# Routed experts: the order of the output weighting and of the inner product's rounding on ACT

## The reference, cut to what matters

```
g = einsum('ech,eih->eci', xb, w_gate)      # 32 experts, 192 rows, 512 -> 256
u = einsum('ech,eih->eci', xb, w_up)
inter = silu(g) * u                         # the inner product's operand
yb = einsum('eci,ehi->ech', inter, w_down)  # 256 -> 512
y = yb[eid, pos] * w_slot[:, None]          # each row weighed by its token's routing weight
routed = y.reshape(-1, K, Hd).sum(axis=1)   # added to the token's row
```

## Time and profile before

| what | us |
|---|---|
| median of 3 runs (1690.84 to 1692.87) | 1692.7 |
| the profiled execution's own time | 1691.99 |
| its span | 1690.2 |
| busy in the span: PE | 1483.3 (88%) |
| busy: DVE | 1112.2 (66%) |
| busy: ACT | 1028.2 (61%) |
| busy: POOL | 767.1 (45%) |

### The profile page before, as it was taken

The page is one execution under the profiler, slowest core; times in us unless marked ns, Lnnn a source line. Parts: engine busy times, 40 slices in busy tenths (PEclk is TensorE's granted clock), DMA queues, the critical chain, the costliest instruction groups (busy, mean ns, idle before and its releaser), DMA issues. The chain is left out here.

```text
span 1690.2 us, 26016 instructions
## 1 busy us (share of the span) xinstructions
PE 1483.3 (88%) x8434; PEld 1232.9 (73%) x8436; DVE 1112.2 (66%) x2284; ACT 1028.2 (61%) x2108; POOL 767.1 (45%) x659
## 2 busy tenths in 40 slices
PE   5999969899994589999999999995999869999994
PEld 4877758777773477887887887774887758778773
DVE  4659857777773256666666675664649857777773
ACT  5762447777773266666667666753762537777773
POOL 0123235555653475666556556420113225556563
PEclk9999979999998789999999999997999989999998
DMA  7736358889994111111111110115655448999994
GB/s 268 239 128 205 107 187 267 253 256 259 266 253 79 64 39 51 38 38 63 38 44 45 63 38 32 32 38 179 212 175 158 139 152 255 269 255 266 268 258 72
DMA packets 94599, 255.57 MB, mean 151 GB/s; under 512 B 19153, under 2 KB 20113, under 8 KB 86193
## 3 DMA queue, kind: packets, MB, share of 16 engines
q1 hardware_dynamic: 71984, 202.58, 35.8%
q0 software_dynamic: 22528, 51.92, 14.4%
HBM read 185.70 MB, written 68.76 MB: 151 GB/s over the span
## 5 line engine op out<-in xcount | busy, mean ns | idle before, releaser
L1032 DVE TENSOR_TENSOR e_w_lo<-e_raw,e_w_hi 128x1024 fp32r<-128x1024 f32 x192 | 233.6, 1218 | 108.7 <-ACT e_w_hi L947 100.5
L947 ACT ACTIVATE e_w_hi<-e_raw 128x1024 fp32r<-128x1024 f32 x192 | 202.6, 1056 | 29.2 <-PEq L270 20.8
L1548 POOL TENSOR_SCALAR t_prob<-t_prob,t_inv 128x128 f32<-128x128 f32 (+7 forms) x128 | 112.0, 875 | 221.7 <-DVE t_inv L1455 221.7
L1122 PE MATMUL e_ps_gate<-e_xt,e_w_hi 128*128 128x384 f32 x512 | 161.3, 378 | 38.6 <-DVE e_w_lo L1032 38.5
L899 POOL DMA_INDIRECT e_xg<-htab,e_gather_idx x128 | 140.0, 1093 | 63.5 <-issue 39.3
L910 POOL DMA_INDIRECT x_after_ffn<-e_y,e_add_idx x64 | 104.4, 1631 | 114.8 <-DMA x_after_ffn<-e_y,e_add_idx 92.1
L910 POOL DMA_INDIRECT out<-e_y,e_add_idx x64 | 104.7, 1637 | 104.3 <-DMA out<-e_y,e_add_idx 83.8
L1122 PE MATMUL e_ps_up<-e_xt,e_w_hi 128*128 128x384 f32 x512 | 151.8, 361 | 0.0
L353 POOL TENSOR_SCALAR d_inter<-d_inter 128x512 f32<-128x512 f32 x32 | 26.5, 827 | 267.8 <-DVE d_inter L518 267.6
L1350 ACT ACTIVATE t_prob<-a_wide,t_neg_max,a_q_scale 128x128 f32<-128x128 f32 (+7 forms) x128 | 106.5, 832 | 54.0 <-DVE t_neg_max L1449 53.8
L1122 PEld LDWEIGHTS e_ps_gate<-e_xt,e_w_hi 128*128 128x128 f32 x512 | 99.0, 193 | 48.6 <-issue 28.9
(11 more groups left out here) (222 smaller groups left out, 4476.9 us busy)
## 6 DMA issues: line engine op xcount, KB each, us to landing
e_raw<-in_w_experts SPq DMA_DIRECT2D x64, 1536.0 KB
htab<-d_h SPq DMA_DIRECT2D x16, 1024.0 KB, 5.3
d_x<-in_x SPq DMA_DIRECT2D x16, 512.0 KB, 6.8
d_xs<-in_x SPq DMA_DIRECT2D x32, 256.0 KB, 3.5
x_after_ffn<-d_xs SPq DMA_DIRECT2D x32, 256.0 KB, 3.2
q_x<-x_after_ffn SPq DMA_DIRECT2D x32, 256.0 KB, 3.1
t_res<-x_after_ffn SPq DMA_DIRECT2D x32, 256.0 KB, 2.6
x_after_attention<-t_res SPq DMA_DIRECT2D x32, 256.0 KB, 2.0
```

What stands on the lines that cost most here:

```text
L947: act.activation(w_hi[u][:, cols], raw[u][:, cols], ACT.Copy).then_inc(hi_ready, 1)
L1032: dve.tensor_tensor(w_lo[u][:, cols], raw[u][:, cols], w_hi[u][:, cols].bitcast(F32), ALU.subtract).then_inc(lo_ready, 1)
L1122: pe.matmul(out, w[0][:, c, cols], xt[u][:, c, :, :], start=c == 0, stop=False)
L1548: pool.tensor_scalar(prob[:, u, 0:width(i)], prob[:, u, 0:width(i)], inv[:, u:u + 1], 1.0, ALU.mult, ALU.mult).then_inc(p_ready, 1)
```

## The change

On ACT the weighting of the outputs of the expert behind moves ahead of the rounding of the inner product. `weigh` gets a parameter that could do the halves separately; both calls give it both halves. Nothing is added or left out, and no other engine's stream changes.

```diff
-                def weigh(i, u):
+                def weigh(i, u, halves):
                     e = 2 * i + u
-                    act.wait_ge(y_free, e + 1)
-                    act.wait_ge(col_done, e + 1)
-                    act.activation(add_idx[u][:, :], slots[:, bass.ds(2 * e, 2)], ACT.Copy)
-                    for q in range(2):
+                    if 0 in halves:
+                        act.wait_ge(y_free, e + 1)
+                        act.wait_ge(col_done, e + 1)
+                        act.activation(add_idx[u][:, :], slots[:, bass.ds(2 * e, 2)], ACT.Copy)
+                    for q in halves:
                         act.wait_ge(d_ready, 2 * e + q + 1)
...
                     gate(i, u)
                     unload_up(i, u)
+                    if behind:
+                        weigh(pi, nu, (0, 1))
                     split_inner(i, u)
-                    if behind:
-                        weigh(pi, nu)
                     if ahead:
                         split(ni, nu, 2)
...
-                weigh(E // 2 - 1, 1)
+                weigh(E // 2 - 1, 1, (0, 1))
```

## The result

The changed kernel takes 1711.97 us (median of 4 runs, 1708.39 to 1718.31), the kernel before 1692.51 (median of 4, 1690.84 to 1692.87). The ratio is 1.0108, 95% interval 1.0091 to 1.0126: slower by 1.1%, where 1.5% faster was forecast, and outside the stated range. The profiled execution took 1709.90 us, its span is 1708.1 us, 17.9 us longer than before.

A forecast was written before the change was run, and what follows sets the result against it. It took the ACT-DVE ring, 8.97 us a step, as the bound; with DMA-limited steps of 8.70 us, 8.8 + 6.7 + 9.7 = 25.2 us come off 1691.99, giving 1666.8, plus 0.7: 1667.5 us. Range 1648 to 1690.

The forecast's parts named there:

- The ring: ACT and DVE waiting on each other in the routed experts: 8.97 us a step, 7.73 without the weighting's 1.24.
- the chain: POOL's scatters, each starting only when the one before has landed: present pace 9.10 us a step.
- The three waits: ACT's waits for PE's down product, `y_free` and `col_done`, moved ahead of the rounding: costed at nothing, 1.7 us of room.
- PE's own step: What PE alone needs for a routed expert's step, waits for weights and rows taken off: 8.37 us.
- The DMA step: Weights 4.4 us plus scatters and gathers 4.1 us, together 8.56 a step; 8.70 with 0.14 for late loads.
- The step that failed: Routed experts: the step becomes the longest of ring 7.73, PE 8.37, and what DMA engines and scatter chain allow.
- PE as the bound: Rival, chance 0.20: DMA work packs better, a routed expert's step is 8.37 us, 42.7 us saved, 1650.0 us.
- The chain keeps its pace: Rival, chance 0.24: POOL's scatters can't go below 9.05 us, only attention-chunk steps win, 1686.0 us.
- The slower one: Rival, chance 0.10: weighting waits at `y_free` ahead of the rounding, loads start late, steps 9.32 us, 1700.3 us.
- The first rival's rule: One core may draw about 435 GB/s, so a step's 2.39 MB take 5.5 us and DMA bounds nothing.

The follow-up runs named there:

- e4: Changed kernel with POOL's gather for expert e + 2 issued ahead of the scatter of e - 3, not behind it: 1755.4 us.
- e5: Changed kernel without its scatter-adds, so the routed sum is missing from the output: 1605.8 us.
- e12: Kernel before without its scatter-adds, so the routed sum is missing from the output: 1661.1 us.
- e6: Changed kernel loading only the first half of each expert's weights from the third expert on, all instructions kept: 1622.8 us.
- e3: Changed kernel with four extra matmuls a step on PE, ahead of each expert's turns: 1688.2 us.
- e10: Changed kernel with one half of the outputs weighed ahead of the rounding and the other behind it: 1704.5 us.
- e9: Changed kernel with odd experts' scatters in the second layer adding to another table, so a scatter waits for the one two before: 1687.7 us.
- e11: Changed kernel with three extra matmuls a step on PE (0.70 us): 1692.5 us.

## Why the prediction was wrong, point by point

**The ring** was right. It is no longer the bound, the rounding stands straight behind the outputs, the short steps of e4 are 7.72 us where 7.73 was forecast for the ring, and e5 and e12 give 55 us for it without the chain.

**The three waits** were costed at nothing, by room that isn't there. The room of 1.7 us at `d_ready` was read at the pace of before, when the ring held PE back. Now PE is the slower of the two, ACT waits for the down product 56 times, and the rounding comes up to 0.36 us later than the product in most of the short steps and 1.6 to 1.7 us in every long one. The forecast had named this as a sign of being wrong (more than 0.1 us). In the short steps it costs nothing, since PE is the bound (e5, e6); e3, with more of it, is faster. What it adds in a long step, where it also holds up the next load, no run separates cleanly; e10, almost without it, has the long steps all the same and takes 1704.5 us.

**PE's own step** was put at 8.37 us and is 8.04 (e5, and the short steps of the changed kernel): too high by 0.33; the idle rows that I took off did not hold all of PE's slack. So PE outran the chain by more than was reckoned with.

**The DMA step** was put at 8.56, and 8.70 with late loads. Without the serial landing wait it is 8.82 (e9); with it, steps of 8.75 still end in stalls (e11) and 8.97 to 8.99 hold (e3). The size was off by 0.1 to 0.3, which alone would have left the change a gain.

**The step that failed** is "the step becomes the longest of ring 7.73, PE 8.37, and what the DMA engines and the scatter chain allow". That holds if a faster stage that waits for a slower one waits without loss. Here the wait falls on PE, since the gathers stand in POOL's stream behind scatters that wait for landings, and PE's clock pays for it: 3.4 us of standing, then 3.1 us at 0.50. And while PE catches up, the next load isn't asked for and the DMA engines idle. So the average isn't the slowest member's pace, 8.8 or 9.0, but 9.44 to 9.56. The kernel before had its slow member, the ring at 8.97, in the right place: it spread PE's wait over the steps, in pieces that were mostly under 0.8 us.

**The rivals.** PE as the bound: no. The chain keeps its pace: it named late rows, but without the loss behind a stall, 1686. The slower one had the sign right, was nearest (1700.3) and had the mechanism in part: ring and PE outrun the chain and stall. Its place was wrong. `y_free` held ACT once, for 2.7 us in all, and the rows held PE for 77.9 us. In the waits of ACT over the whole changed kernel (us in total, times, longest):

```profile
ACT e_y L980 <- PE e_ps_down L89: 37.6, 56, 2.3
...
ACT e_w_hi L947 <- DMA e_raw<-in_w_experts: 19.8, 16, 2.6
...
ACT e_add_idx L977 <- POOLq L907: 2.7, 1, 2.7
```

I had written against it that a wait for something the chain does anyway doesn't lengthen the chain. It did: the mean distance of scatter starts went from 8.96 to 9.29 in the second layer. The five steps of 9.32 that I quoted for it already gave nearly the size: at 9.32 throughout it would have been 1700.3, measured are 9.56 and 9.44.

**The first rival's rule.** The highest rate over a long stretch of this stage was 271 GB/s, at a share of 0.93 (e9). By the Trainium skill, page "Perfetto Trace Analysis", section "Roofline", one core may draw about 435 GB/s; no long stretch of this stage came near it.

**What stays open.** How the loss of the whole stage divides between the clock and the idle DMA engines. In the step shown, the standing and the clock account for PE's time, but with the clock up PE might only have caught up sooner and stood longer for the next rows. The clock can be summed: (1 - 0.946) x 1708.1 = 92.2 us of full-speed time missing, before (1 - 0.962) x 1690.2 = 64.2, so 28 us more, which is more than the 17.9 us lost; but not all of it was on the path, and no run kept the clock up through a stall. Nor was it tried why gathers land late when a load is started close behind them (10.3 us above); that the load is the cause is argued from the traces and from e6, where halved loads leave no late gather.

## What to carry to other kernels

Before a stage is made faster, ask which other member of the loop runs at nearly its pace, and which engine will do the waiting when it is overtaken. Where that is PE, a wait of some microseconds every few steps costs twice, by itself and by the lower clock behind it; a slower but even pace can be the faster kernel. A useless filler on the engine that leads is a cheap test for this: if the time falls, the pace was the trouble.

## What the runs showed of the hardware that I had not expected

Within 0.7 us behind 3.39 us without a matmul the granted clock fell to 0.50, for 3.1 us of full work, and a gate matmul that takes 0.36 us at a granted clock of 1.00 took 0.57 to 0.67. Adding four matmuls a step to the busiest engine made the changed kernel 1.4% faster (1712.0 to 1688.2), with no change to what it computes. A pair of gathers that landed in 4.5 to 7.6 us in the kernel before needed more than 9 us in half of the changed kernel's steady steps.
